# One stage for the long convolution and the expert logits of a decoder layer on one Trainium2 core

## The reference, cut to what matters

```python
kv = einsum('bhil,bhjl->bijhl', ctx, ctx)       # 32 heads of 8 channels, 512 long
y = causal_convolution(kv, ssm_kernel) + kv * D
x = x + einsum('bijhl,bhil->bjhl', y, layernorm(x))   # called q below
xn = layernorm(x)
logits = xn @ Wr + br                            # 512 -> 12 experts, top 3
```

## Time and profile before

| what | value |
|---|---|
| median of 3 runs | 1633.63 us (1633.26 to 1633.86) |
| the profiled execution's own time | 1632.18 us |
| its span, first to last instruction | 1630.4 us |
| mean granted TensorE clock | 0.936 of full |
| PE busy | 1461.7 us, 90% of the span |
| DVE busy | 795.1 us, 49% |
| ACT busy | 661.3 us, 41% |
| POOL busy | 823.0 us, 50% |

### The profile page before, as it was taken

The page is one execution under the profiler, slowest core; times in us unless marked ns, Lnnn a source line. Parts: engine busy times, 40 slices in busy tenths (PEclk is TensorE's granted clock), DMA queues, the critical chain, the costliest instruction groups (busy, mean ns, idle before and its releaser), DMA issues. The chain is left out here.

```text
span 1630.4 us, 27973 instructions
## 1 busy us (share of the span) xinstructions
PE 1461.7 (90%) x7638; PEld 1113.4 (68%) x7639; DVE 795.1 (49%) x1098; ACT 661.3 (41%) x1789; POOL 823.0 (50%) x892
## 2 busy tenths in 40 slices
PE   3899999589997841999999999999999999999956
PEld 1555555357775741888888888888888888888842
DVE  3456656448888568734717443473471734000003
ACT  0545555423322130444444444544444445444420
POOL 2444555044442001576766766767666667565530
PEclk9999999989998555999999999999999999999977
DMA  6000000022233540634525433454452543241115
GB/s 243 3 1 0 0 0 1 1 74 89 83 86 113 208 161 13 188 91 110 142 64 159 106 104 100 103 161 109 103 157 50 160 103 77 50 123 32 26 23 215
DMA packets 75260, 148.08 MB, mean 91 GB/s; under 512 B 8864, under 2 KB 13472, under 8 KB 74720
## 3 DMA queue, kind: packets, MB, share of 16 engines
q1 hardware_dynamic: 59232, 110.36, 21.2%
q0 software_dynamic: 14320, 35.40, 10.6%
q10 hardware_dynamic: 1680, 1.97, 0.4%
HBM read 115.11 MB, written 32.59 MB: 91 GB/s over the span
## 5 line engine op out<-in xcount | busy, mean ns | idle before, releaser
L1481 PE MATMUL ps_h<-w_hi,xh 128*128 x708 | 250.5, 365 | 1.4 <-ACT xh L1407 1.4
L1482 PE MATMUL ps_h<-w_lo,xh 128*128 x708 | 246.0, 359 | 0.0
L1504 PE MATMUL ps_y<-w_hi,hh 128*128 x590 | 240.0, 407 | 4.4 <-issue 4.4
L1309 DVE TENSOR_TENSOR w_lo<-stage,w_hi 128x512 f32 x220 | 224.0, 1018 | 27.0
L1505 PE MATMUL ps_y<-w_lo,hh 128*128 x590 | 233.8, 396 | 0.0
L1360 POOL TENSOR_TENSOR y<-y,b_sb 128x512 f32<-128x512 f32 x59 | 80.6, 1366 | 229.6 <-ACT y L1432 229.6
L1353 POOL TENSOR_TENSOR hl<-h,hh 128x1280 fp32r<-128x1280 f32 x59 | 188.2, 3189 | 15.1 <-ACT hh L1426 15.1
L763 PE MATMUL ps_b<-kv,toe 128*128 128x320 f32 x640 | 175.2, 437 | 6.9 <-POOL kv L724 6.9
L1486 PE MATMUL ps_h<-w_hi,xl 128*128 x708 | 167.0, 357 | 0.0
L1413 ACT ACTIVATE h<-ps_h 128x512 f32<-128x512 f32 x177 | 80.6, 527 | 209.2 <-POOL hl L1353 200.8
L763 PEld LDWEIGHTS ps_b<-kv,toe 128*128 128x128 f32 x640 | 123.1, 192 | 58.9 <-issue 9.2
(11 more groups left out here) (204 smaller groups left out, 2321.2 us busy)
## 6 DMA issues: line engine op xcount, KB each, us to landing
stage<-in_wcat SPq DMA_DIRECT2D x220, 256.0 KB, 3.0
toe<-kpad SPq DMA_DIRECT2D x32, 256.0 KB, 3.2
cc<-in_ctx_rev SPq DMA_DIRECT2D x32, 192.0 KB, 3.1
w_lo<-in_wcat SPq DMA_DIRECT2D x4, 1280.0 KB, 11.5
acc<-zeros POOLq DMA_DIRECT2D x1, 4352.0 KB, 18.1
xs<-in_x SPq DMA_DIRECT2D x4, 1024.0 KB, 13.3
x2d<-xs SPq DMA_DIRECT2D x4, 1024.0 KB, 8.3
xnd<-xn_c SPq DMA_DIRECT2D x16, 256.0 KB, 2.0
```

The source lines that it names most:

```text
L1309: nc.vector.tensor_tensor(lo, stage[:, c % NSTAGE], hi.bitcast(F32), ALU.subtract).then_inc(split_done, 1)
L1481: nc.tensor.matmul(out, x_hi, part(w_hi, e, k * FF + lo, hi - lo), start=(k == 0), stop=False)
L1482: nc.tensor.matmul(out, x_hi, part(w_lo, e, k * FF + lo, hi - lo), start=False, stop=False)
L1504: nc.tensor.matmul(ps_y[:], h_hi, part(w_hi, e, KD * FF + k * D, D), start=(k == 0), stop=False)
```

## The change

`logits_phase` is gone; its work is part of `convolution`, and every hardware loop in it is written out.

- `kv` holds 36 columns a batch, every pair of channels once: 32 for distances 0 to 3 and 4 for distance 4, from two POOL instructions. The ten matmuls stream 288 columns and write 36 of every 64 columns of a bank. ACT copies in three instructions. DVE's three instructions are as before.
- The 28 columns left free of every 64 take other results. Tiles are renumbered: n = 0 to 7 are the first halves of the batches, whose sums are ready after 16 heads, n = 8 to 15 the second halves. From head 18 on, every second head, PE transposes the sums of one tile into the gaps, ACT copies them to SBUF (`added`), DVE adds them after its work on the head, and takes statistics and aggregate. POOL raises the variance to the power -0.5 in four small instructions (`inverse_std`), ACT normalises, PE transposes xn into the gaps of the other banks, and ACT copies it to `xT`, of which eight are kept. Tiles 0 to 6 are summed so within the heads, and 0 to 4 are transposed.
- The rest runs after the heads in a fixed order, with two banks for sums and two for xn.
- Logits: `Wr`, padded to 32 columns, is the stationary operand, and xT moves. Four tiles go to four groups of 32 output partitions of one bank (16 matmuls), ACT copies the bank, one transpose turns it, and one DVE instruction takes four tiles.
- SP stores x and xn tile by tile in the same queue as the taps. `acc` is zeroed from POOL's queue after the fourth head.

```diff
--- before.py
+++ after.py
...
@@ -31,6 +31,12 @@
 CE = CH + ND - 1
 WRAP = CH - ND
 YE = (WRAP + CH) * ND
+NEAR = CH * (ND - 1)
+FAR = CH // 2
+NPAIR = NEAR + FAR
+SPAN = 512 // B
+HALF = SH // 2
+GROUP = 4
 NKV = 4
 QE = 2 * CH
 KPAD = 640
...
-
         def sem(name):
             return ctx.enter_context(nc.semaphore(name))
 
-        NCOL = B * ND * CH
+        NCOL = B * NPAIR
         toe = sb("toe", [P, 2, D])
...
+        br_sb = sb("br_sb", [P, E])
+        xn = sb("xn_c", [P, 2, D])
+        xT = sb("xT_c", [P, B, KD * P])
+        added = sb("added_c", [P, D])
+        lT = sb("lT", [P, P])
+        zeros = added
+        ps = ctx.enter_context(nc.psum_tensor("ps_b", [P, 8, 512], F32))
 
         toe_in = [sem("toe_in0"), sem("toe_in1")]
         cc_in = [sem("cc_in0"), sem("cc_in1")]
         kv_ready = sem("kv_ready")
...
+        xt_done = sem("xt_done_c")
+        xt_evac = sem("xt_evac_c")
+        lt_done = sem("lt_done")
...
+        def token_tile(n):
+            return TPB * n if n < B else TPB * (n - B) + 1
+        IN_SUMS, IN_TURNED = 7, 5
+        def gap_view(half):
+            return view(ps[:], half * LB * 512 + NPAIR, [[512, LB], [SPAN, B], [1, P // B]])
+        def gap_slot(half, l):
+            return view(ps[:], (half * LB + l) * 512 + NPAIR, [[SPAN, B], [1, P // B]])
+        def sums_slot(n, l):
+            return gap_slot(0, l) if n < IN_SUMS else ps[:, n % 2, l * P:(l + 1) * P]
+        def turned_slot(n, k):
+            return gap_slot(1, k) if n < IN_TURNED else ps[:, 2 + n % 2, k * P:(k + 1) * P]
+        def split_row(ap):
+            return view(ap, 0, [[P, LB], [P // B, B], [1, P // B]])
+        lt, lg = ps[:, 4], ps[:, 5]
...
+            def store(n):
+                rows = slice(token_tile(n) * P, (token_tile(n) + 1) * P)
+                sp.wait_ge(x2_ready, n + 1)
+                sp.dma_start(x2d[rows], xs[:, token_tile(n)]).then_inc(x2_out, 16)
+                sp.wait_ge(xn_ready, n + 1)
+                sp.dma_start(xnd[rows], xn[:, n % 2]).then_inc(xn_out[n % 2], 16)
...
+            stored = 0
+            for h in range(2, SH):
+                load_toe(h)
+                if h + 1 < SH:
+                    load_cc(h + 1)
+                if h == HALF + 7 + 2 * stored:
+                    store(stored)
+                    stored += 1
+            for n in range(stored, NT):
+                store(n)
...
+            def multiply(h):
+                pool.wait_ge(cc_in[h % 2], 16 * (h // 2 + 1))
+                if h > 2:
+                    pool.wait_ge(prod_ready, h - 2)
+                if h >= NKV:
+                    pool.wait_ge(conv_done, h - NKV + 1)
+                buf = h % NKV
+                c = cc[:, h % 2]
                 nc.gpsimd.tensor_tensor(
-                    view(kv[:, buf], 0, [[ND * CH, LB * B], [ND, CH], [1, ND]]),
-                    view(c, 0, [[CE, LB * B], [1, CH], [0, ND]]),
-                    view(c, 0, [[CE, LB * B], [1, CH], [1, ND]]), ALU.mult).then_inc(kv_ready, 1)
-
-            for h in range(NKV):
-                multiply(h, h, h == NKV - 1)
-            with pool.Fori(1, SH // NKV) as i:
-                for buf in range(NKV):
-                    multiply(NKV * i + buf, buf, True)
+                    view(kv[:, buf], NEAR, [[NPAIR, LB * B], [1, FAR]]),
+                    view(c, 0, [[CE, LB * B], [1, FAR]]),
+                    view(c, FAR, [[CE, LB * B], [1, FAR]]), ALU.mult)
+                nc.gpsimd.tensor_tensor(
+                    view(kv[:, buf], 0, [[NPAIR, LB * B], [ND - 1, CH], [1, ND - 1]]),
+                    view(c, 0, [[CE, LB * B], [1, CH], [0, ND - 1]]),
+                    view(c, 0, [[CE, LB * B], [1, CH], [1, ND - 1]]), ALU.mult).then_inc(kv_ready, 1)
+            def inverse_std(n):
+                pool.wait_ge(aggr, n + 1)
+                r = rstd[:, n:n + 1]
+                nc.gpsimd.tensor_scalar(r, mv[:, n, 1:2], EPS, None, ALU.add).then_inc(scaled, 1)
+                pool.wait_ge(scaled, 2 * n + 1)
+                nc.gpsimd.tensor_tensor(r, r, power[:], ALU.pow).then_inc(rstd_ready, 1)
+                pool.wait_ge(rstd_ready, n + 1)
+                m = nmr[:, n:n + 1]
+                nc.gpsimd.tensor_tensor(m, mv[:, n, 0:1], r, ALU.mult).then_inc(scaled, 1)
+                pool.wait_ge(scaled, 2 * n + 2)
+                nc.gpsimd.tensor_scalar(m, m, -1.0, None, ALU.mult).then_inc(nmr_ready, 1)
+            nc.gpsimd.memset(wr_sb[:], 0.0)
+            nc.gpsimd.memset(power[:], -0.5)
+            nc.gpsimd.memset(zeros[:], 0.0).then_inc(zeroed, 1)
+            pool.wait_ge(zeroed, 1)
+            for h in range(SH):
+                multiply(h)
+                if h == NKV - 1:
+                    pool.dma_start(acc.rearrange("(t p) d -> p t d", p=P), view(zeros[:], 0, [[0, NT + 1], [1, D]]))\
+                        .then_inc(acc_out, 16)
+                n, odd = divmod(h - HALF - 5, 2)
+                if 0 <= n and not odd:
+                    inverse_std(n)
+            for n in range((SH - HALF - 4) // 2, NT):
+                inverse_std(n)
+            pool.wait_ge(acc_out, 16)
...
-            with act.Fori(0, SH // 2) as i:
-                evacuate(2 * i, 0)
-                evacuate(2 * i + 1, 1)
+            def evacuate(h):
+                par, near = h % 2, ND - 1
+                act.wait_ge(conv_done, h + 1)
+                if h > 1:
+                    act.wait_ge(prod_ready, h - 1)
+                for at, src, n in ((0, (CH - WRAP) * near, WRAP), (WRAP * ND, 0, CH)):
+                    nc.scalar.activation(
+                        view(ye[:, par], at, [[YE, LB * B], [ND, n], [1, near]]),
+                        view(ps[:], 4 * par * 512 + src, [[SPAN, LB * B], [near, n], [1, near]]), ACT.Copy)
+                nc.scalar.activation(
+                    view(ye[:, par], WRAP * ND + near, [[YE, LB * B], [FAR * ND, 2], [ND, FAR]]),
+                    view(ps[:], 4 * par * 512 + NEAR, [[SPAN, LB * B], [0, 2], [1, FAR]]), ACT.Copy)\
+                    .then_inc(ye_ready, 1)
+            def normalise(n):
+                act.wait_ge(nmr_ready, n + 1)
+                if n > 1:
+                    act.wait_ge(xt_done, n - 1)
+                    act.wait_ge(xn_out[n % 2], 16 * (n // 2))
+                nc.scalar.activation(xn[:, n % 2], xs[:, token_tile(n)], ACT.Identity, bias=nmr[:, n:n + 1],
+                                     scale=rstd[:, n:n + 1]).then_inc(xn_ready, 1)
+            def evac_x(n):
+                act.wait_ge(xt_done, n + 1)
+                if n >= B:
+                    act.wait_ge(lt_done, n // GROUP - 1)
+                if n < IN_TURNED:
+                    ins = nc.scalar.activation(split_row(xT[:, n % B]), gap_view(1), ACT.Copy)
+                else:
+                    ins = nc.scalar.activation(xT[:, n % B], ps[:, 2 + n % 2], ACT.Copy)
+                ins.then_inc(xt_evac, 1)
+                return ins
...
+            def evac_sums(n):
+                act.wait_ge(rt_done, n + 1)
+                if n:
+                    act.wait_ge(x2_ready, n)
+                else:
+                    act.wait_ge(acc_out, 16)
+                nc.scalar.activation(split_row(added[:]), gap_view(0), ACT.Copy).then_inc(added_ready, 1)
+            def evac_lt(g):
+                act.wait_ge(lt_done, g + 1)
+                if g:
+                    act.wait_ge(logit_done, g)
+                nc.scalar.activation(lT[:], lt[:, 0:P], ACT.Copy).then_inc(lt_evac, 1)
+            for h in range(SH):
+                evacuate(h)
+                n, odd = divmod(h - HALF - 2, 2)
+                if 0 <= n and not odd:
+                    evac_sums(n)
+                m, odd = divmod(h - HALF - 7, 2)
+                if 0 <= m and not odd:
+                    evac_x(m)
+                n, odd = divmod(h - HALF - 4, 2)
+                if 0 <= n and not odd:
+                    normalise(n)
+            evac_x(5)
+            normalise(6)
+            evac_lt(0)
+            evac_x(6)
+            normalise(7)
+            evac_x(7)
+            normalise(8)
+            evac_lt(1)
+            for n in range(8, 12):
+                normalise(n + 1)
+                evac_x(n)
+            evac_lt(2)
+            for n in range(12, NT):
+                if n + 1 < NT:
+                    normalise(n + 1)
+                evac_x(n)
+            evac_lt(3)
...
+            def free_banks(h):
+                if h > 1:
+                    pe.wait_ge(ye_ready, h - 1)
+                n, odd = divmod(h - HALF - 4, 2)
+                if 0 <= n < IN_SUMS and not odd:
+                    pe.wait_ge(added_ready, n + 1)
+                n, odd = divmod(h - HALF - 9, 2)
+                if 0 <= n < IN_TURNED and not odd:
+                    pe.wait_ge(xt_evac, n + 1)
+            def convolve(h):
+                par, buf = h % 2, h % NKV
+                pe.wait_ge(toe_in[par], 16 * (h // 2 + 1))
```

(109 more changed lines are left out.)

278 lines of the change are left out of this document (60 added, 218 removed).

## The result

The changed kernel takes 1591.24 us (median of 4 runs, 1589.77 to 1592.59) against 1633.70 beside it: ratio 0.974, 95% interval 0.9723 to 0.9757. Its profiled execution took 1590.10 us, span 1588.1, against 1632.18 and 1630.4: 42.1 us less.

A forecast was written before the change was run, and what follows sets the result against it. PE was taken to bound the heads and logits, DVE the sums. Gains of 1.0 us in the heads and 38.3 after them, 39.3 together, gave 1592.9 profiled and a 1594 us median; 8-in-10 range 1585 to 1606.

The forecast's parts named there:

- straight code instead of loops I cost at nothing: Convolution: writing out the hardware loops was given no time effect, since no profile row prices it.
- The bound moves from PE to DVE: Heads: DVE becomes the bound, so only 0.42 of the 0.54 us PE saves a head arrive.
- 32 x 4.97: Heads: 32 heads at a DVE-bound period of 4.97 us, 159.0 us in all, before the tiles' 12.3.
- I charge nothing, and 3 us at the most: Heads 4 to 7: zeroing `acc` beside them, 4.35 MB in 18 us, costs nothing, at most 3 us.
- half of each overlapped microsecond: Heads: POOL and DVE sharing SBUF, at full strength, costs 0.1 us a head or 3 us in all.
- I take half: After the heads: PE's clock taken as half for transposes and logits, a four-tile logits group costing 2.1 us.
- Rival A: After the heads: full clock cuts 31.1 us to 24; with heads at 4.87, 1585 to 1589 us; chance 0.15.
- The prediction's own argument: Logits: attention's 32 records of 0.27 us each fit in 1.08, agreeing with up to 4x from packing.
- main case: Whole kernel: 1589 to 1601 us around the forecast of 1594; chance 0.60.
- B: Slower rest: `inverse_std` at 2.9 us adds 5, heads at 5.1 add 4, waits 5; 1602 to 1609 us; chance 0.17.
- C: Heads: period stays 5.39 us and seven tile adds come on top, +13.4; 1608 us; chance 0.05.
- D: Last 14 heads: PE idles and its clock falls, 4.7 us lost a head, up to 1660 us; chance 0.03.

The follow-up runs named there:

- run 1: Kernel before the change with only the 36 pair columns (two POOL products, three ACT copies), hardware loops and separate stages kept: 1625.56 us, ratio 0.9954.
- run 2: Kernel before the change with the 36 pair columns and every convolution loop written out, stages still separate: 1615.45 us, ratio 0.9894.
- run 3: Changed kernel with all 16 tiles summed, normalised and turned after the heads, none between them: 1592.89 us, ratio 0.9756.
- run 9: Changed kernel with DVE adding the epsilon, so POOL has two small instructions a tile instead of four: 1589.83 us, ratio 0.9740.
- run 5: Changed kernel with `acc` zeroed in 17 transfers, one after each of POOL's first 17 products, instead of one: 1587.90 us, ratio 0.9720.
- run 6: Changed kernel with POOL's `inverse_std` behind the next head's product and ACT's normalise one head later: 1590.66 us, ratio 0.9743.
- run 4: Changed kernel with the old logits form: xT stationary, 12 columns of `wr` moving, no logits copy or last transpose: 1606.94 us, ratio 0.9844.
- run 7: Changed kernel with 11 added matmuls of 512 columns on PE whose result nobody reads: 1589.17 us, ratio 0.9724.
- run 8: Changed kernel with PE transposing sums one tile further ahead, before the waiting transposes of xn: 1587.00 us, ratio 0.9718.

## Why the prediction was right, point by point

It said 1594 and 39.3 us of gain; the profiled execution gained 42.1. By parts, as timed: the columns 7.8 (run 1), the loops 10.1 (run 2), the stages made one with four tiles a logits group and POOL's powers 22.6 (run 3), the tiles in the heads 1.7 (across two sets of runs, within their scatter). The mechanism and its place were right: the heads end about where they did and carry seven tiles, and the gain lies behind them. Several terms were not, and that the sum came so near is in part luck: the heads took 2.3 us more than forecast, the rest 3.7 less, and DVE's first head started at 344.35 for 345.4, at the low end of what the runs show.

**The heads, 171.3 us forecast, 173.6 measured.** The step "straight code instead of loops I cost at nothing" failed, on the good side. I took the 0.14 us between DVE's instructions as a gap that stays; written out it is 0.04. The 0.52 us in front of its product I read as waiting for PE, and for the kernel before that is so:

```profile
473.23 1.73 ACT L743 ACTIVATE ye<-ps_b 128x480 f32<-128x480 f32 x2 [3.66 <-PE ps_b L763]
```

`ye` was there at 474.96, after DVE's reduction (474.59) and just before its product at 475.10. But under that wait lay the loop's own cost, 0.23 and 0.52 us in run 1: with the columns alone DVE needs 5.24 us a head on average, and 0.14 of PE's 0.54 arrives. "The bound moves from PE to DVE" also failed. Written out, DVE needs about 4.8 us a head (457.70 to 462.49 in run 9, where PE isn't waited for), under PE's 4.85: up to the tiles PE stays the bound, and all of its 0.54 arrives. That is 3.8 us less than 32 x 4.97. "I charge nothing, and 3 us at the most" for the zeroing failed on the other side: 4.1 us (run 5). Tap loads still land in 3.3 us by the median of 32; a median says nothing of the two that met the large transfer, and I gave the clock no part in it. The tiles cost 13.7 us for 12.3 (run 3): 1.55 each for 1.75 since the gaps are 0.03 to 0.04, and on top the five products of 2.3. Sum: -3.8 + 4.1 + 1.4 = +1.7 of the 2.3; where the other 0.6 lies no run shows.

**The contention was weighed and left too small.** I let POOL's product reach 0.2 us into DVE's next one, and took half of each overlapped microsecond as its full price. That half comes from the earlier trace rows, 1018 ns for 693, and was too small: in the heads with tiles POOL's product reached 0.94 us in and cost 0.81, and in run 6 an add of 0.69 lost 0.8, while DVE's reduction, which has one operand in SBUF, stays at 2.29 with POOL's product on it. The other direction was not weighed at all: POOL's 128x1 instruction takes 1.37 us beside the product and 0.21 alone (519.66 in the changed kernel). The Trainium skill, "GPSIMD Engine Reference", section "Specifications", says that POOL contends with DVE instructions of two SBUF inputs. The trace agrees with it in all four numbers.

**The rest, 31.1 us forecast, 27.4 measured.** Two terms share the 3.7 us, and no run parts them exactly. One is the price of a tile, 1.55 for 1.75, which is 1.8 over nine tiles. The other is "I take half" for the clock: from 527.4 to about 541 it was full, in work like that which kept it at half before. Run 4 tells part of why: with the 12-column logits back in this order it stayed at half to 538, was full among transposes from 539 to 545, and fell again in the next group. It doesn't tell which property of them it is. Rival A's 24 us for full clock throughout was a good price: run 7 took 24.6. Against the other prices: inverse 1.5 for 1.7, normalise 0.81 for 0.65, group 1.94 at half as forecast (2.1) and 1.08 at full. The last aggregate ends 20.4 us after the last reduction for 23.6: nine tiles 14.0, three logits reads 0.5, and waiting for PE's order 5.7 for 8. The last chain took 7.0 for 7.5. The order as the cost of the adds is confirmed by run 8, which takes the waits to 0.5 us.

**The logits.** 16 records at half clock took 3.59 us; a group of four tiles with 32 records 1.94. Run 4's group against the changed kernel's, 7.0 to 1.94 at the same clock, is 3.6 to 1, but run 4 also changes which operand stands still, so this is the price of the two forms and not of packing. For packing there is an estimate: the heads' records of 288 columns are 0.243 us apart (4.85 over 20), so 32 records of 128 columns one behind another would take 3.5 us at full clock; the group took 1.08, 3.2 to 1. The Trainium skill's "TensorEngine Tiling (Array Packing)", section "Theoretical Speedup", gives up to 4x, and the estimate agrees. The prediction's own argument does not carry it: 32 records of 0.27 us in 1.08 would be 8 to 1, since 0.27 is a record's length and not its distance from the next. Of the 20 us of PE work that I counted as saved (16 x 1.8 less 4 x 2.1), run 4 shows 15.9 on the path, with DVE's 1.91 and the clock in it.

**The rivals.** A was half right: the clock was full for part of the rest, and the time, 1591.2, lies between the 1594 of the main case and A's 1585 to 1589. B fell for the rest: the inverse in the PE order took 1.5 us. In the heads it took 3.4 (442.69 to 446.05), which is what made POOL's product late. C fell: the period is 4.84. D fell: the windows of the heads show 1.00 with PE busy 126.6 of 130 us, and the only dip, 0.72, is the zeroing's.

## What to carry to other kernels

A DVE instruction that waits on its own engine inside a hardware loop pays for the loop: before a period is called bound by DVE's work, take the loop's gaps out of it, and price "loop written out" by the gaps inside a turn and at it. A wait for another engine can lie over such a gap and hide it. Between two engines that share SBUF access, leave out small instructions of the one beside two-input instructions of the other: the edit that only shifted them (run 6) moved the loss. Putting them beside the reduction suggests itself; it wasn't tried here. Split a large transfer that has time to spare when loads with a deadline lie beside it, and look at the worst load, not the median.

## What the runs showed of the hardware

From a head's reduction to the next product DVE stood 0.52 us at the loop's turn and 0.23 inside it (run 1), and 0.03 written out (run 9). One transfer of 4352 KB from POOL's queue held the 16 DMA engines at a share of 1.01 to 1.03 for 12 us, and PE waited 2.15 us for a load beside it; the clock then fell in the changed kernel's profile and not in run 7's, and DVE stood 4.22 and 2.55 us; in 17 pieces PE was never idle in the first heads (run 5). A POOL instruction of one element a partition took 1.37 us beside a DVE product, 0.21 alone, and a DVE product that met POOL's ended 1.38 us after it. The granted clock came back to full at 527.4 us in narrow work, after 5.4 us of transposes and one logits group in which PE was never idle, and stayed there to 541 with PE busy 57% of 528 to 540. With 12-column matmuls among the same transposes it was at half from 519 to 538, though PE was never idle from 528 on (run 4).
